# A gated cross-attention and MoE block: residual biases moved into causal steps, norm offsets by one GpSimd product with means that VectorE negates

## The chip, the cores and the metric

The kernel runs on one core of one Trainium2 chip. The metric is the device time of one launch in microseconds (us). TensorE is called PE, VectorE DVE, ScalarE ACT, GpSimd POOL, SyncE SP.

## The reference

For each of 32 sequences of 128 rows and 128 features, in float32:

```python
x = x + tanh(g_x) * attention(layernorm(x), ctx, ctx)        # 16 heads of 8, every row sees every key
x = x + tanh(g_f) * ffn(layernorm(x))
# ffn(y):
q, k = rope(y) @ Wq.T + bq, rope(y) @ Wk.T + bk;  v = y @ Wv.T + bv
x1 = layernorm(y + causal_attention(q, k, v) @ Wo.T + bo) * ln1_w + ln1_b
gates = softmax(x1 @ gate_w.T + gate_b); take the two largest of 8
moe = sum over these two of gate * (x1 @ expert_w.T + expert_b)
return layernorm(x1 + moe) * ln2_w + ln2_b
```

The change touches the two norms inside ffn (the first before ln1_w, the second before ln2_w) and the addition of tanh(g_f) * ln2_b to the residual x.

## The kernel before

**Stages.** Sequences are taken in pairs ("groups", G = 2, GROUPS = 16). A unit is a pair in one of the two attentions: units 0 to 15 are the cross attention of groups 0 to 15, units 16 to 31 the causal attention. A unit has eight tiles (TILES), of four heads of one sequence each. One loop over slots n, written out for every engine, runs both: slot n makes the scores of tile n; step s = n // 8, t = n % 8. Causal step k is step 16 + k. Maxima, exponentials and products with the values follow at fixed lags, and the inputs of a unit are prepared two to four steps ahead. The last slots (DRAIN = 257 and eight more, two tiles in each) empty the pipeline. Then comes the last stage (functions z_...): steps of its own, s = 3 to 21, in which group s gets its output projection and first norm, group s-1 its logits, group s-2 gates and experts, group s-3 its second norm. Each engine runs its own list in a fixed order, written by hand in its body function; semaphores count finished instructions. Groups 0 and 1 and a part of 2 are started earlier, in the functions early(n), between the last slots of the attention.

**POOL in a causal step** (pool_attention, L350 to L383): at t = 0 the four instructions of max_split (L338 to L344) that split the maxima of one sequence into bf16 parts, which PE transposes two slots later (L509), and the same at t = 4; at t = 1 second_row (L284) and the first product of the rotation (L303), which waits for DVE's first_row (L684); at t = 2 two more (L307); at t = 3 the attention bias (L317); at t = 5 and 6 middle_part (L322), which waits for DVE's rests (L697), rotate step 3 (L313) and low_part (L327); at t = 7 the deviation with a power (L277, L280). After these, early(n) is called in each slot.

**Where the residual biases are.** x_all holds the residual x. z_pool's early (L1370) multiplies the rows l2w and l2b by tanh(g_f) at slot DRAIN - 18 = 239 (L1373, two instructions, 128x128) and adds l2b to x_all of one group in each of the slots 240 to 255 (L1377, 128x256 each). The pair of x_all is last read by the causal attention three steps before the unit's own step.

**The two norms.** DVE adds the projection from PSUM to the input (attention_add, L1126), takes statistics (L1133) and moments (L1139: mean and variance). POOL's factor1 (L1334) makes v + eps (L796), its power -1/2 (L798, a tensor_tensor of 128x2 with a tile of -0.5), and then, for groups from 2 on, the offset -mean * rstd in one tensor_scalar for each sequence (L1342, 128x1). ACT's normalise1 (L1035) applies rstd as scale and the offset as bias. For groups 0 and 1 DVE normalises (L1145) from mean and rstd and no offset is made; PE transposes the result (transpose_n, L897), POOL multiplies and adds ln1_w and ln1_b (L1313, L1318). The second norm is alike: experts_add (L1225), statistics and moments (L1233, L1239), factor2 on POOL (L1345, offsets L1353), normalise2 on ACT (L1026), then final on POOL (L1326: times l2w, L1332: plus x_all) and a store by SP. The last two groups are closed by DVE: weigh (L1250) and close (L1259), without offsets.

**The other names.** DVE: maxima L716, shift_logits L1158 and L1161, gated_pairs L1208, gating with L1182 and L1184, gated_sum L1215, experts L1199. ACT: copy_x1 L1018 (transposed x1), gate_experts L1059. PE: logits L909, experts L923, gated_sum L942 and L944, transposes L897, project L886. DVE's and POOL's orders in a step of the last stage are those of the two functions body (L1262, L1356).

## Time and profile before

| | |
|---|---|
| device time, three runs | 441.07, 441.62, 441.66 us; median 441.62 |
| the profiled execution's own time | 441.23 us |
| its span | 439.4 us |
| PE busy | 385.7 us (88%) |
| DVE busy | 369.2 us (84%) |
| POOL busy | 323.3 us (74%) |
| ACT busy | 288.4 us (66%) |
| granted TensorE clock | 0.998 of full speed |

Times inside the profile count from the span's start. A timeline row gives start, duration, engine, line, operation, the tile written and the tiles read with their shapes, and how many instructions are merged in it; in brackets stands the idle time before it and what ended it. The causal attention runs from about 150 to 330 us, the last stage from about 333 us to the end.

### The profile page before, as it was taken

How to read it: one execution, taken by the hardware profiler on the slowest of the kernel's cores; microseconds unless marked ns; L12 is line 12 of the kernel's file. 1: busy time of each engine (PE TensorE's matmuls, PEld its weight loads, DVE VectorE, ACT ScalarE, POOL GpSimd, SP SyncE). 2: the span in 40 equal slices, each digit the busy share in tenths (PEclk: the TensorE clock that was granted, in tenths of full speed). 3: DMA queues.
4: the chain of work that ended last, by engine and by line, in shares of the span. 5: the costliest groups of instructions: out<-in, count | busy, mean ns of one | idle time of the engine just before them, and what ended most of it. 6: DMA issues, size and time to landing. Idle time of an engine off the chain costs nothing.

```text
span 439.4 us, 17671 instructions
## 1 busy us (share of the span) xinstructions
PE 385.7 (88%) x6538; PEld 231.3 (53%) x6538; DVE 369.2 (84%) x1188; ACT 288.4 (66%) x728; POOL 323.3 (74%) x740
## 2 busy tenths in 40 slices
PE   0368888888888899999999999999999999999994
PEld 0134544454444555666666666666655555555541
DVE  6587999999997878888878878877848999999987
ACT  1126777767766766666666666666665788788772
POOL 4456767767778988888888788849823788888884
PEclk9999999999999999999999999999999999999999
DMA  6855686685553333333434343333000000000001
GB/s 163 193 155 160 170 199 169 162 180 145 132 158 101 98 100 105 104 106 104 109 106 125 103 127 100 99 105 96 12 4 2 1 25 13 24 27 12 25 25 48
DMA packets 88037, 42.76 MB, mean 97 GB/s; under 512 B 16000, under 2 KB 87824, under 8 KB 87952
## 3 DMA queue, kind: packets, MB, share of 16 engines
q1 hardware_dynamic: 80864, 39.59, 34.2%
q10 hardware_dynamic: 7088, 2.04, 2.0%
q8 instruction: 53, 0.87, 0.8%
q14 instruction: 32, 0.26, 0.2%
HBM read 5.69 MB, written 2.10 MB: 18 GB/s over the span
## 4 chain that ended last, share of the span: by engine, by line
PE 41%; DVE 6%; ACT 5%; issue 3%; POOL 1%; SPq 1%; DMA 1%; POOLq 0%; ACTq 0%; DVEq 0%
PE s_bank L923 6%; PE u_bank L499 6%; PE st_bank L923 6%; PE s_bank L421 4%; PE s_bank L434 3%; DVE r L697 2%; PE t_bank L413 2%; PE u_bank L944 2%; PE u_bank L942 2%; PE u_bank L909 2%; PE t_bank L407 2%; ACT z_x_t L1018 2%; ACT part L577 1%; PE u_bank L514 1%; PE t_bank L408 1%
## 5 line engine op out<-in xcount | busy, mean ns | idle before, releaser
L716 DVE TENSOR_REDUCE nm<-s_bank 128x4 f32<-128x512 f32 x256 | 171.5, 683 | 36.3 <-PE s_bank L434 34.0
L599 ACT ACTIVATE pt<-st_bank 128x512 f32<-128x512 f32 x250 | 147.5, 602 | 74.0 <-PE st_bank L434 51.6
L434 PE MATMUL s_bank<-qk 64*64 64x128 bf16 (+1 forms) x1584 | 103.5, 220 | 12.1 <-DVE nm L716 5.7
L499 PE MATMUL u_bank<-pt,vaug 128*32 128x128 f32 x2048 | 108.3, 286 | 1.6 <-DVE ao L733 0.2
L434 PE MATMUL st_bank<-qk 64*64 64x128 bf16 (+1 forms) x1540 | 98.2, 218 | 0.0
L434 PEld LDWEIGHTS s_bank<-qk 64*64 64x64 bf16 (+1 forms) x1584 | 73.8, 104 | 36.1 <-issue 18.9
L434 PEld LDWEIGHTS st_bank<-qk 64*64 64x64 bf16 (+1 forms) x1540 | 69.1, 103 | 0.0
L499 PEld LDWEIGHTS u_bank<-pt,vaug 128*32 128x32 f32 x2048 | 41.1, 108 | 27.5 <-issue 5.2
L421 PE MATMUL s_bank<-mqk,idb 64*64 64x256 bf16 x256 | 38.3, 292 | 0.8 <-ACT pt L599 0.4
L327 POOL TENSOR_TENSOR part<-r,part 128x512 bf16<-128x512 f32 x32 | 37.1, 1158 | 1.4
L421 PE MATMUL st_bank<-mkq,idb 64*64 64x256 bf16 x244 | 35.7, 293 | 0.0
L606 ACT ACTIVATE mts<-m_bank 128x128 bf16<-128x128 bf16 x63 | 17.5, 278 | 24.9 <-PE m_bank L509 24.9
L514 PE MATMUL u_bank<-idf,us 128*128 128x128 f32 x128 | 28.0, 300 | 5.2 <-ACT us L615 4.9
L1059 ACT ACTIVATE z_gated<-st_bank,z_gates 128x128 f32<-128x128 f32 x120 | 32.3, 381 | 0.0
L923 PE MATMUL s_bank<-ewt,z_x_t 128*128 128x512 f32 x64 | 31.4, 613 | 0.0
L923 PE MATMUL st_bank<-ewt,z_x_t 128*128 128x512 f32 x64 | 30.2, 594 | 0.0
L338 POOL TENSOR_SCALAR mst<-nm 128x16 bf16<-128x16 f32 x64 | 13.0, 203 | 23.2 <-DVE nm L716 22.9
L322 POOL TENSOR_SCALAR part<-r 128x512 bf16<-128x512 f32 x32 | 19.8, 617 | 13.5 <-DVE r L697 7.3
L421 PEld LDWEIGHTS s_bank<-mqk,idb 64*64 64x64 bf16 x256 | 14.3, 103 | 24.5 <-issue 13.8
L1199 DVE SCALAR_TENSOR_TENSOR z_acc<-s_bank,z_gates,z_acc 128x128 f32<-128x128 f32 x96 | 26.1, 342 | 0.0
L798 POOL TENSOR_TENSOR z_rstd<-z_ve,mhalf 128x2 f32<-128x2 f32 x32 | 23.7, 741 | 2.7
L280 POOL TENSOR_TENSOR rstd<-ve,mhalf 128x2 f32<-128x2 f32 x32 | 22.8, 711 | 2.7
(136 smaller groups left out, 815.4 us busy)
## 6 DMA issues: line engine op xcount, KB each, us to landing
qk<-part SPq DMA_DIRECT2D x221, 128.0 KB, 2.8
x_all<-x SPq DMA_DIRECT2D x16, 128.0 KB, 2.6
qk<-qrow SPq DMA_DIRECT2D x32, 64.0 KB, 2.0
c_all<-ctx_in SPq DMA_DIRECT2D x14, 128.0 KB, 2.8
out<-z_o SPq DMA_DIRECT2D x14, 128.0 KB, 1.8
qk<-mts ACTq DMA_DIRECT2D x34, 32.0 KB, 2.7
qk<-mts SPq DMA_DIRECT2D x30, 32.0 KB, 2.1
ewt<-exp_t SPq DMA_DIRECT2D x1, 512.0 KB
```

Of the source, the lines that this page charges most:

```text
L280: pool.tensor_tensor(rstd[u % 2][:, :], ve[u % 2][:, :], mhalf[:, :], ALU.pow).then_inc(rstd_s, 1)
L327: pool.tensor_tensor(part[u % 2][:, 2:2 * PARTS:PARTS, :], r32[:, :].rearrange("c (o t) -> c o t", o=2), part[u % 2][:, 1:2 * PARTS:PARTS, ...
L421: pe.matmul(to, idb[rows, rows], mask[rows, rows].unsqueeze(1).broadcast_to([64, HEADS, 64]), start=True, stop=False, skip_group_check=True)
L434: ins = pe.matmul(to[outs, :], fixed[:, outs], moving, start=not masked, stop=True, skip_group_check=masked)
L499: ins = pe.matmul(u_bank[b][32 * j:32 * j + 32, r * P:(r + 1) * P], v, pt[m % 4][:, j, :], start=half == 0, stop=half == 1, skip_group_che ...
L514: ins = pe.transpose(u_bank[q % 2][:, W + r * P:W + (r + 1) * P], us[q % 2][:, r * P:(r + 1) * P], idf[:, :])
L599: act.activation(pt[m % 4][:, :, :].rearrange("k j q -> k (j q)"), transposed_bank(m)[:, :], ACT.Exp).then_inc(ex, 1)
L716: dve.tensor_reduce(nm[q % 2][:, first:first + HEADS], s_bank[n % 2][:, :].rearrange("q (j k) -> q j k", j=HEADS), AX_X, ALU.max, negate=T ...
L798: pool.tensor_tensor(r_out, v_eps, mhalf[:, :], ALU.pow).then_inc(semaphore, 1)
L923: ins = pe.matmul(e_bank[b][k][:, :], zx1t[i][:, b * P:(b + 1) * P], ewt[:, k * 512:(k + 1) * 512], start=True, stop=True)
L1059: ins = act.activation(zyg[:, b, e, :], e_bank[b][1][:, e * P:(e + 1) * P], ACT.Copy, scale=zg[i][:, b, HALF + e:HALF + e + 1])
L1199: dve.scalar_tensor_tensor(out=zacc[i][e % 2][:, b, :], in0=e_bank[b][0][:, e * P:(e + 1) * P], scalar=zg[i][:, b, e:e + 1], in1=zacc[i][( ...
```

## The change

The addition of l2b to x_all goes from slots 240 to 255 into earlier ones: groups 0 to 8 at t = 0 of causal steps 4 to 12 (slots 160, 168, ... 224), groups 9 to 13 in slots 232 to 236 (causal step 13), groups 14 and 15 in slots 242 and 246 (step 14). The two products that make l2w and l2b go from slot 239 to slot 152 (causal step 3). DVE gets a new instruction after the moments of each first norm, and of each second norm but the last group's: tensor_scalar of the two means (128x2) by -1 into a new tile. POOL's two tensor_scalars for the offsets become one tensor_tensor of 128x2, negated means times rstd. factor1, factor2 and weigh wait for all instructions on their semaphores, the new one among them. The counts on the semaphores are adapted (H1 and ALL from 5 to 6; the rstd counts from 4 to 3 for each group).

```diff
--- before.py
+++ after.py
@@ -801,7 +801,7 @@
             return [sb(f"{name}{i}", shape) for i in range(2)]
         zo_t = two("z_att_t", [P, W])
         zh = two("z_h", [P, G, P])
-        zst = two("z_stats", [P, G, 6]); zmv = two("z_mv", [P, G, 2]); zve = two("z_ve", [P, G]); zrs = two("z_rstd", [P, G]); znb = two("z_offset", [P, G])
+        zst = two("z_stats", [P, G, 6]); zmv = two("z_mv", [P, G, 2]); zve = two("z_ve", [P, G]); zrs = two("z_rstd", [P, G]); znb = two("z_offset", [P, G]); zmn = two("z_minus_mean", [P, G]); zmn2 = two("z_minus_mean2_", [P, G])
         zn = two("z_n", [P, G, P])
         zw = sb("z_nw", [P, G, P]); zx1 = two("z_x1", [P, G, P])
         zx1t = two("z_x1_t", [P, W])
@@ -822,10 +822,10 @@
         z_gtc = sem("z_gates_t_copied"); z_y = [sem(f"z_experts{k}") for k in range(2)]; z_yg = sem("z_experts_gated"); z_yp = sem("z_gated_pairs_summed"); z_yq = sem("z_gated_summed"); z_yb = sem("z_expert_bias")
         z_acc = sem("z_accumulated"); z_all = sem("z_all_summed_steps"); z_rs2 = sem("z_rstd2_steps"); z_y2s = sem("z_normalised2")
         z_fin = sem("z_final_steps"); z_xb = sem("z_residual_biased"); z_yw = sem("z_weighted"); z_yo = sem("z_closed_by_vector"); z_out = sem("z_stored"); z_tail = [sem(f"z_tail_stored{i}") for i in range(2)]
-        H1 = 1 + 2 * G
+        H1 = 2 + 2 * G
         GATE = 11
         ACC = G * HALF
-        ALL = 1 + 2 * G
+        ALL = 2 + 2 * G
         FIN = 2
         LAST = GROUPS - 1
 
@@ -840,7 +840,10 @@
             return (u_bank[0] if g else t_bank)[:, first:first + G * NE]
 
         def rstd_steps(g):
-            return 2 * g if g <= 2 else 4 * g - 4
+            return 2 * g if g <= 2 else 3 * g - 2
+
+        def all_steps(g):
+            return (g + 1) * ALL - (1 if g == LAST else 0)
 
         def in_z(c, lag):
             return 0 <= c - lag < GROUPS
@@ -1019,7 +1022,7 @@
                                scale=l1wc[:, :]).then_inc(z_x1c, 1)
 
             def normalise2(g, gc):
-                act.wait_ge(z_rs2, (g + 1) * 4)
+                act.wait_ge(z_rs2, (g + 1) * 3)
                 if gc >= 2:
                     act.wait_ge(z_fin, (g - 2) * FIN + 1)
                 for b in range(G):
@@ -1138,6 +1141,12 @@
                 for b in range(G):
                     dve.bn_aggr(zmv[i][:, b, :], zst[i][:, b, :]).then_inc(z_h, 1)
 
+            def attention_minus_mean(g, gc):
+                i = gc % 2
+                dve.wait_ge(z_h, (g + 1) * H1 - 1)
+                dve.tensor_scalar(zmn[i][:, :], zmv[i][:, :, 0], -1.0, 0.0, ALU.mult, ALU.add).then_inc(z_h, 1)
+
+
             def normalise1(g, gc):
                 i = gc % 2
                 dve.wait_ge(z_rs, 2 * (g + 1))
@@ -1149,6 +1158,7 @@
                 attention_add(g, gc)
                 attention_stats(g, gc)
                 attention_moments(g, gc)
+                attention_minus_mean(g, gc)
 
             per_seq = [P, G, NE]
 
@@ -1238,21 +1248,28 @@
                 for b in range(G):
                     dve.bn_aggr(zmv2[g % 2][:, b, :], zst2[g % 2][:, b, :]).then_inc(z_all, 1)
 
+            def experts_minus_mean(g, gc):
+                if g < LAST:
+                    dve.wait_ge(z_all, (g + 1) * ALL - 1)
+                    dve.tensor_scalar(zmn2[g % 2][:, :], zmv2[g % 2][:, :, 0], -1.0, 0.0, ALU.mult, ALU.add).then_inc(z_all, 1)
+
+
             def all_experts(g, gc):
                 experts_add(g, gc)
                 experts_stats(g, gc)
                 experts_moments(g, gc)
+                experts_minus_mean(g, gc)
 
             def weigh(g):
                 i = g % 2
-                dve.wait_ge(z_all, (g + 1) * ALL)
+                dve.wait_ge(z_all, all_steps(g))
                 for b in range(G):
                     dve.scalar_tensor_tensor(out=zyc[i][:, b, :], in0=zsum[i][:, b, :], scalar=zmv2[i][:, b, 0:1],
                                              in1=l2w[:, :], op0=ALU.subtract, op1=ALU.mult).then_inc(z_yw, 1)
 
             def close(g):
                 i = g % 2
-                dve.wait_ge(z_rs2, (LAST - 1) * 4 + (i + 1) * 2)
+                dve.wait_ge(z_rs2, (LAST - 1) * 3 + (i + 1) * 2)
                 dve.wait_ge(z_yw, (i + 1) * G)
                 dve.wait_ge(z_xb, GROUPS)
                 for b in range(G):
@@ -1275,6 +1292,8 @@
                     experts_stats(s - 3, c - 3)
                     attention_moments(s, c)
                     experts_moments(s - 3, c - 3)
+                    attention_minus_mean(s, c)
+                    experts_minus_mean(s - 3, c - 3)
                 elif in_z(c, 3):
                     all_experts(s - 3, c - 3)
                 if in_z(c, 3):
@@ -1307,6 +1326,12 @@
             return early, steps
 
         def z_pool(pool):
+            FIRST_BIAS = (GROUPS + 4) * TILES
+
+            def last_bias(g):
+                pool.tensor_tensor(zpair(x_all, g), zpair(x_all, g), l2b[:, :].unsqueeze(1).broadcast_to([P, G, P]),
+                                   ALU.add).then_inc(z_xb, 1)
+
             def x1(g, gc):
                 i = gc % 2
                 pool.wait_ge(z_n, (g + 1) * G)
@@ -1337,21 +1362,18 @@
                 if gc >= 2:
                     pool.wait_ge(z_n, (g - 1) * G)
                 rstd_of(pool, zmv[i][:, :, 1], zve[i][:, :], zrs[i][:, :], z_rs, rstd_steps(g))
-                for b in range(G if g >= 2 else 0):
+                if g >= 2:
                     pool.wait_ge(z_rs, rstd_steps(g) + 2)
-                    pool.tensor_scalar(znb[i][:, b:b + 1], zmv[i][:, b, 0:1], zrs[i][:, b:b + 1], -1.0,
-                                       ALU.mult, ALU.mult).then_inc(z_rs, 1)
+                    pool.tensor_tensor(znb[i][:, :], zmn[i][:, :], zrs[i][:, :], ALU.mult).then_inc(z_rs, 1)
 
             def factor2(g, gc):
                 i = g % 2
-                pool.wait_ge(z_all, (g + 1) * ALL)
-                k = g * 4 if g < LAST else (LAST - 1) * 4 + 2
+                pool.wait_ge(z_all, all_steps(g))
+                k = g * 3 if g < LAST else (LAST - 1) * 3 + 2
                 rstd_of(pool, zmv2[i][:, :, 1], zve2[i][:, :], zrs2[i][:, :], z_rs2, k)
                 if g < LAST - 1:
                     pool.wait_ge(z_rs2, k + 2)
-                    for b in range(G):
-                        pool.tensor_scalar(znb2[i][:, b:b + 1], zmv2[i][:, b, 0:1], zrs2[i][:, b:b + 1], -1.0,
-                                           ALU.mult, ALU.mult).then_inc(z_rs2, 1)
+                    pool.tensor_tensor(znb2[i][:, :], zmn2[i][:, :], zrs2[i][:, :], ALU.mult).then_inc(z_rs2, 1)
 
             def body(s, c):
                 if in_z(c, 1):
@@ -1368,14 +1390,17 @@
                     factor2(s - 3, c - 3)
 
             def early(n):
-                if n == DRAIN - 18:
+                if n == FIRST_BIAS - TILES:
                     for t in (l2w, l2b):
                         pool.tensor_scalar(t[:, :], t[:, :], tg[:, 1:2], 0.0, ALU.mult, ALU.add).then_inc(c_l2, 1)
                     pool.wait_ge(c_l2, 2)
-                g = n - DRAIN + 17
-                if 0 <= g < GROUPS:
-                    pool.tensor_tensor(zpair(x_all, g), zpair(x_all, g), l2b[:, :].unsqueeze(1).broadcast_to([P, G, P]),
-                                       ALU.add).then_inc(z_xb, 1)
+                g, t = divmod(n - FIRST_BIAS, TILES)
+                if 0 <= g < 9 and t == 0:
+                    last_bias(g)
+                if g == 9 and t < 5:
+                    last_bias(9 + t)
+                if g == 10 and t in (2, 6):
+                    last_bias(14 + t // 4)
                 if n == DRAIN - 4:
                     factor1(0, 0)
                 if n == DRAIN - 2:
```

## Rows read from the trace of the kernel before

**Rows 1.** Busy us: from:to length, PE, PEld, DVE, ACT, POOL, clock, DMA, GB/s

```profile
210.00:230.00 20.00, 19.42 (x486) 12.69 (x485) 16.08 (x40) 13.36 (x30) 16.19 (x36) 1.00 0.39 105
...
360.21:366.82 6.61, 6.40 (x26) 3.59 (x25) 6.19 (x35) 5.37 (x19) 5.67 (x13) 1.00 0.08 22
```

**Rows 2.** Timeline of PE, last stage: start, us, instruction, [idle before <- releaser]

```profile
372.45 0.61 PE L909 MATMUL u_bank<-gwt,z_x_t 128*128 128x8 f32 x4 [0.21 <-ACT z_x_t L1018]
```

**Rows 3.** Chain that ended last, in order of time: start, us, engine, tile, line

```profile
365.85 0.61 PE u_bank L909 x4
...
370.84 0.63 PE u_bank L944 x2
...
371.83 0.57 ACT z_x_t L1018
```

**Rows 4.** Timeline of POOL, causal step 6 (columns as in rows 2)

```profile
220.59 0.22 POOL L344 TENSOR_TENSOR mst<-mr,mst 128x16 bf16<-128x16 f32 x1
220.80 0.80 POOL L284 TENSOR_SCALAR xn_all<-x_all,mv,rstd 128x128 f32<-128x128 f32 x1
...
222.28 0.72 POOL L303 TENSOR_TENSOR rc<-xn_all,cost 128x256 f32<-128x256 f32 x1 [0.69 <-DVE xn_all L684]
...
226.25 0.62 POOL L322 TENSOR_SCALAR part<-r 128x512 bf16<-128x512 f32 x1 [0.55 <-DVE r L697]
```

**Rows 5.** Timeline of PE, between causal and last stage

```profile
316.31 0.44 PE L897 MATMUL t_bank<-idf,z_n 128*128 128x128 f32 x2 [0.95 <-DVE z_n L1145]
```

**Rows 6.** Timeline of DVE, the same stretch

```profile
315.25 1.00 DVE L1145 TENSOR_SCALAR z_n<-z_h,z_mv,z_rstd 128x128 f32<-128x128 f32 x2
...
320.88 0.59 DVE L1145 TENSOR_SCALAR z_n<-z_h,z_mv,z_rstd 128x128 f32<-128x128 f32 x2
```

**Rows 7.** Timeline of POOL, the same stretch

```profile
314.72 1.45 POOL L1377 TENSOR_TENSOR x_all<-x_all,l2b 128x256 f32<-128x256 f32 x2
```

**Rows 8.** Timeline of DVE, causal step 6

```profile
221.86 0.34 DVE L684 TENSOR_SCALAR xn_all<-x_all,mv,rstd 128x128 f32<-128x128 f32 x1
```

**Rows 9.** Timeline of POOL, causal step 13

```profile
294.45 0.20 POOL L338 TENSOR_SCALAR mst<-nm 128x16 bf16<-128x16 f32 x1 [3.31 <-DVE nm L716]
```

**Rows 10.** Timeline of DVE, last stage: its first and a later step

```profile
334.55 0.68 DVE L1208 TENSOR_TENSOR z_gated_pairs<-z_gated 128x512 f32<-128x512 f32 x1
...
367.59 0.17 DVE L1161 TENSOR_REDUCE z_max<-z_logit 128x2 f32<-128x16 f32 x1
...
367.89 0.69 DVE L1208 TENSOR_TENSOR z_gated_pairs<-z_gated 128x512 f32<-128x512 f32 x1
```

**Rows 11.** Timeline of DVE, the end

```profile
428.40 0.77 DVE L1215 TENSOR_TENSOR z_gated_sum<-z_gated_pairs 128x256 f32<-128x256 f32 x1
429.09 0.69 DVE L1182 TENSOR_TENSOR z_top<-z_exps,z_others 128x16 f32<-128x16 f32 x1
...
433.13 0.25 DVE L1239 BATCH_NORM_AGGREGATE z_mv<-z_stats 128x2 f32<-128x6 f32 x2
433.42 0.61 DVE L1250 SCALAR_TENSOR_TENSOR z_yc<-z_x_moe,z_mv,l2w 128x128 f32<-128x128 f32 x2
```

**Rows 12.** Timeline of POOL, last stage: its first and a later step

```profile
334.73 1.06 POOL L798 TENSOR_TENSOR z_rstd<-z_ve,mhalf 128x2 f32<-128x2 f32 x1
...
367.73 0.70 POOL L798 TENSOR_TENSOR z_rstd<-z_ve,mhalf 128x2 f32<-128x2 f32 x1
368.53 0.50 POOL L1342 TENSOR_SCALAR z_offset<-z_mv,z_rstd 128x1 f32<-128x1 f32 x2
```

**Rows 13.** Lines L1182 and L1215 by source: count, duration min/median/max in ns

```profile
L1182 DVE TENSOR_TENSOR z_top<-z_exps,z_others x16: 166/168/692, 325.5 to 429.1; 128x16 f32<-128x16 f32 x16
...
L1215 DVE TENSOR_TENSOR z_gated_sum<-z_gated_pairs x15: 412/415/765, 335.9 to 428.4; 128x256 f32<-128x256 f32 x15
```

**Rows 14.** Timeline of POOL, the end

```profile
428.16 0.73 POOL L1326 TENSOR_TENSOR z_yw<-z_y,l2w 128x256 f32<-128x256 f32 x1
428.97 0.78 POOL L1332 TENSOR_TENSOR z_o<-z_yw,x_all 128x256 f32<-128x256 f32 x1
```

## The prediction

> **What bounds the kernel now.** The page comes first: TensorE is busy for 88% of the span, VectorE for 84%, GpSimd for 74%. Those are averages, so each stage that the change touches is read by itself.
>
> *Last stage.* One step by the view of busy time [rows 1] lasts 6.61 us; PE is busy for 6.40 of them, DVE for 6.19, ACT for 5.37, POOL for 5.67, at full clock. PE's own timeline has one gap in it [rows 2]: 0.21 us ahead of the logits at L909, until ACT has copied z_x_t. The chain that ended last [rows 3] runs from L909 to L909 in 372.45 - 365.85 = 6.60 us through matmuls and that one copy; nothing of POOL, nothing of the norms. The step is PE's 6.40 plus 0.21. The copy starts when PE's own transposes are done, and these stand in PE's order, which is kept.
>
> *Causal stage.* PE bounds it too, 19.42 us busy in 20 [rows 1]. POOL has two waits in a step [rows 4], 0.69 us before L303 (for DVE's first row, L684) and 0.55 us before L322 (for the rests, L697): 1.24 us to spare in 10.03 us (a step is the distance of equal rows).
>
> *Passage.* At 316.31 PE stands for 0.95 us [rows 5], waiting for DVE's z_n (L1145). DVE was working all along: it reached L1145 at 315.25 and took 1.00 us for the two [rows 6]; the same two at 320.88 took 0.59. The difference, 0.41 us, falls while POOL runs two residual biases (314.72, 1.45 us) [rows 7].
>
> **The change, part by part.**
>
> *Biases moved, causal steps 4 to 12.* Nine TENSOR_TENSORs of 0.72 us (1.45 / 2, rows 7) go behind the first maxima split of a step. Before, L344 starts at 220.59 and L284 directly behind it; now L284 starts about 0.7 later, at 221.5, and ends at 222.3. DVE's L684 [rows 8] was done at 222.20 and L303 waited for it until 222.28. So the 0.69 gap swallows the bias, if L684 isn't held. L684 starts at 221.86, when L284 is now at work; z_n beside the biases shows that a tensor_scalar of DVE can be held. Held to L284's end, it finishes 0.35 us later, about 222.55; L303 starts 0.35 late, and the 0.55 gap before L322 takes that. Of 1.24 us, 0.72 + 0.35 = 1.07 are used. PE doesn't notice. Cost taken: 0; bounds 0 and, if the cover were gone, the whole excess in each of nine steps (second rival). The Trainium skill ("SBUF — State Buffer", Who interferes with whom) states that VectorE in a 2-port mode, or with two SBUF inputs against a reading GpSimd instruction, and GpSimd exclude each other for the whole instruction. By it the hold here is certain rather than possible, and the sum is the same 0, since the figure above already holds L684 to the end of L284.
>
> *Causal step 13.* Five biases, 3.6 us. Four lie in the 3.31 us for which POOL waits before the split at 294.45 [rows 9], 2.9 us. The fifth lies between a split and L322, where rows 4 have 0.55 us: at most 0.17 late, once. The stacks' issues on SP follow two more instructions of POOL; I take 0, bound +0.17. *Step 14:* two biases and the l2w, l2b pair (moved to slot 152, where it stands in a causal step as a bias does, two instructions with half the elements each) leave a stretch in which POOL ran without a pause and PE too. Nothing on SP's queue is moved past; the moved work issues no DMA. 0.
>
> *What leaves the passage.* The sixteen biases, the last of them up to 316.2 [rows 7], are gone from here. POOL is idle beside z_n(0), so the pair takes 0.59 instead of 1.00: -0.41. PE waits for exactly this (0.95 us), and what follows on PE and on POOL (L1313, then the last maxima split) follows z_n.
>
> *VectorE's negated means.* Nothing shows a 128x2 tensor_scalar on DVE. Nearest rows: L1161, which writes 128x2, takes 0.17 [rows 10]. With the 0.04 us by which a waiting DVE instruction follows the one before (L1239 ends at 433.38, L1250 starts at 433.42) [rows 11] that is 0.21. Lower bound 0, if it slips into a wait; upper bound twice that, 0.42. I take 0.21, as the shape is the same. Where it counts:
> - Step 0 in the passage: it stands between the moments of group 0 and the maxima and z_n behind them on DVE, which run without idle up to 315.25 [rows 6]: +0.21. POOL's rstd comes 0.21 later too, still ahead of z_n. So PE gets z_n(0) at -0.41 + 0.21 = **-0.20**.
> - Steady steps: two of them, the first hidden behind the second moments' pipeline, so about 0.25 us in all, in front of L1158 and L1161. L1161 ended at 367.76 and L1208 started at 367.89, when ACT's z_gated was there. DVE is busy for 6.19 of 6.61 us: 0.42 to spare. The maxima of the logits come 0.2 later, so do ACT's exponentials, and DVE's chain gives at most 0.05, before z_h (L1126), which waits for PE anyway. 0 per step.
> - The end: weighing of group 14 (L1250) waits one more instruction, on the path that ends: **+0.21**.
>
> *GpSimd's product.* Two tensor_scalars of 128x1, 0.50 us together [rows 12], become one tensor_tensor of 128x2. Nearest row: L344's tensor_tensor of 128x16, 0.22 [rows 4]; from above, L798 at the same shape with a power, 0.70 (bounds 0.2 and 0.7). I take 0.22: -0.28 per norm. But the rstd now waits for the negated mean, +0.2, so that the first offsets come about when they did (369.03), and the second some 0.3 earlier. Behind them stand ACT's normalisations, z_n which PE transposes only behind L944 (370.84 [rows 3]). In steady steps nothing of it reaches PE: 0.
>
> There is a trap in it. The power at L798 starts at 367.73 and L1208 (two SBUF inputs) at 367.89, and neither is stretched; at 334.73 L1208 had begun first (334.55 [rows 10]), and the same power took 1.06 [rows 12]. With L796 0.2 later the power comes behind L1208: +0.36 on POOL. By the skill's rule above one of the two would have to wait for the other in every step; rows 10 and 12 show both at their usual length when the power is first, so here the measurement decides. POOL has 0.9 us to spare in a step, so 0 either way.
>
> *The end.* L1215 and L1182 took 0.77 and 0.69 us at 428.40 and 429.09 [rows 11], against medians of 0.415 and 0.168 [rows 13]. They end where POOL's L1326 (428.16 + 0.73) and L1332 (428.97 + 0.78) end or get going [rows 14]: DVE is held by GpSimd's last products. These follow the offsets of group 13; these come 0.28 earlier with one product (0.2 of it certain), and L1182 is released that much earlier: **-0.22**.
>
> **Sum:** -0.20 (passage) - 0.22 + 0.21 (end) = -0.2 us. The profiled execution took 441.23 us (span 439.4 and 1.8 around it), 0.39 below the median of the runs, 441.62. On its own scale that is 441.0; on the median's 441.4.
>
> **Rivals.**
> - *The holds at the end go altogether* (L1215 and L1182 at their medians: -0.36 - 0.52 = -0.88 instead of -0.22), and ACT's copy of group 15 comes 0.12 earlier: -0.20 - 0.88 - 0.12 + 0.21 = -1.0, 440.6. For it: POOL is earlier. Against it: L1326 and L1332 back to back last 1.5 us, and an advance of 0.3 doesn't carry them past DVE.
> - *The hold in the causal steps outgrows its cover*: place, L684 behind the bias; price, whatever the bias and the hold take beyond 1.24 us, as the parts, the rstd and the next maxima split then come late and PE waits at L509. It decides from 0.17 us more hold than I charge. At 0.2 us of excess, nine steps give +1.8: 443.2, slower. For it: z_n(0) was held though the first bias had ended. Against: behind L284 POOL waits for L684 itself, so nobody can hold it further.
> - *The relief doesn't come* (L1145 takes 1.00 for another reason): +0.21 instead of -0.20, and with +0.21 - 0.22 at the end 441.8: no difference that shows.
> - *DVE becomes the bound of the last stage*: from 0.42 us for the two new instructions on. At 0.3 each, 0.18 over in 13 steps: +2.3, 443.9. Against: nothing that small takes 0.3 on DVE.
>
> **How the numbers follow.** Forecast 0.58, holds gone 0.14, cover outgrown 0.07, no relief 0.16, DVE bound 0.05. A measurement of this kernel tells 0.2% (0.88 us) from nothing. Faster by more: most of the second case, 0.12. Slower by more: the third and the fifth, 0.12. Within: 0.76. The range goes from the second case, 440.6, to "no relief" with twice the price of the negated means (+0.21 at both places) and 0.17 in step 13, 442.3; the two slow cases, 0.12, stay outside.
>
> **What would show it.** Right: L1145 at 0.59 in its first pair, PE's wait at L897 0.75 instead of 0.95; equal distances of L909 in the last stage; L303's wait near 0 and L322's at 0.2 with steps of 10.03; L1182 released some 0.2 earlier; new DVE rows of some 0.17. Wrong: a causal step longer than 10.03, idle time of PE at L509 behind L344, or a last-stage step other than 6.60.

## The result, and the profile after

The changed kernel takes 442.53 us (median of 9 runs, 442.03 to 442.77), the one before 441.13 on the same chip (9 runs, 440.81 to 441.66); the ratio is 1.0025 with a 95% interval of 1.0016 to 1.0034. So it is slower, by 0.16 to 0.34%, and 442.53 lies 0.23 us above the range. The profiled execution took 442.59 us with a span of 440.8 (before 441.23 and 439.4). Ratios here and below are given with their 95% interval; they are estimates over all runs and differ a little from the quotient of two medians, which is 1.0032 here.

The change shifts the line numbers. What was L897, L909, L923 and L1018 is L900, L912, L926 and L1021 in the changed kernel; DVE's L1182, L1199, L1208, L1215 and L1225 are L1192, L1209, L1218, L1225 and L1235; POOL's L1342 and L1353 are L1367 and L1376, its L1326 and L1332 are L1351 and L1357. L1332 is now the residual bias, and L1225 the sum of gated pairs.

**Causal stage.** POOL's timeline of step 6 in the changed kernel; compare [rows 4].

```profile
220.12 0.22 POOL L344 TENSOR_TENSOR mst<-mr,mst 128x16 bf16<-128x16 f32 x1
220.29 0.72 POOL L1332 TENSOR_TENSOR x_all<-x_all,l2b 128x256 f32<-128x256 f32 x1
221.01 0.85 POOL L284 TENSOR_SCALAR xn_all<-x_all,mv,rstd 128x128 f32<-128x128 f32 x1
222.00 0.72 POOL L303 TENSOR_TENSOR rc<-xn_all,cost 128x256 f32<-128x256 f32 x1
...
225.77 0.62 POOL L322 TENSOR_SCALAR part<-r 128x512 bf16<-128x512 f32 x1 [0.35 <-DVE r L697]
```

The bias (L1332) stands where L284 stood, L303's wait of 0.69 is gone and 0.35 is left before L322. DVE's first row (L684) is not held, as the same step of DVE's timeline shows: it starts while L284 is at work and takes 0.34 us, as before. L284 took 0.85 instead of 0.80. The step is 10.03 us long as before.

```profile
221.38 0.34 DVE L684 TENSOR_SCALAR xn_all<-x_all,mv,rstd 128x128 f32<-128x128 f32 x1
```

**Passage.** PE's and DVE's timelines there; compare [rows 5, 6].

```profile
315.82 0.44 PE L900 MATMUL t_bank<-idf,z_n 128*128 128x128 f32 x2 [0.59 <-DVE z_n L1154]
```

```profile
313.41 0.17 DVE L1147 TENSOR_SCALAR z_minus_mean<-z_mv 128x2 f32<-128x2 f32 x1
315.17 0.59 DVE L1154 TENSOR_SCALAR z_n<-z_h,z_mv,z_rstd 128x128 f32<-128x128 f32 x2
```

Both terms are there: z_n is down from 1.00 to 0.59, and a negated mean of 0.17 stands in front of it. From the matmuls of project(0) to the transposes of z_n(0) PE needs 5.47 us instead of 5.67.

**Last stage.** The distance of one step's logits from the next was 6.60 us in the steady steps (the first took 6.50, the last 6.47). In the changed kernel 6.76 and 6.60 take turns. Rows of one long step, from all engines, around the norms and the logits that end it (compare [rows 2, 10, 12]):

```profile
367.23 0.15 DVE L1147 TENSOR_SCALAR z_minus_mean<-z_mv 128x2 f32<-128x2 f32 x1
...
367.47 0.19 POOL L796 TENSOR_SCALAR z_ve<-z_mv 128x2 f32<-128x2 f32 x1 [0.92 <-DVE z_minus_mean L1147]
...
367.71 0.69 DVE L1218 TENSOR_TENSOR z_gated_pairs<-z_gated 128x512 f32<-128x512 f32 x1
...
367.75 1.22 POOL L798 TENSOR_TENSOR z_rstd<-z_ve,mhalf 128x2 f32<-128x2 f32 x1
...
369.04 0.48 POOL L1367 TENSOR_TENSOR z_offset<-z_minus_mean,z_rstd 128x2 f32<-128x2 f32 x1
369.05 0.41 DVE L1225 TENSOR_TENSOR z_gated_sum<-z_gated_pairs 128x256 f32<-128x256 f32 x1
...
369.90 0.69 POOL L798 TENSOR_TENSOR z_rstd<-z_ve,mhalf 128x2 f32<-128x2 f32 x1
...
370.67 0.20 POOL L1376 TENSOR_TENSOR z_offset<-z_minus_mean,z_rstd 128x2 f32<-128x2 f32 x1
...
370.89 0.88 ACT L1029 ACTIVATE z_y<-z_x_moe,z_offset,z_rstd 128x128 f32<-128x128 f32 x2 [0.20 <-POOL z_offset L1376]
...
371.68 0.25 ACT L1052 ACTIVATE z_gates_t<-u_bank 16x128 f32<-16x128 f32 x1
371.84 0.54 ACT L1021 ACTIVATE z_x_t<-t_bank,l1bc,l1wc 128x256 f32<-128x256 f32 x1
...
372.43 0.39 PE L912 MATMUL u_bank<-gwt,z_x_t 128*128 128x8 f32 x2 [0.37 <-ACT z_x_t L1021]
```

Read it from top to bottom. v+eps (L796) waits for the negated mean, so the power starts 0.04 us behind DVE's L1218, and takes 1.22 us instead of 0.70. The product then starts as DVE's L1225 does, and takes 0.48. The second norm follows in POOL's order. Its product ends at 370.87, which is 5.20 us behind the logits (at 365.67) instead of 4.90. ACT's z_y was waiting for it. Behind z_y stand, in ACT's order, the copies of the gates and of x1, and PE waits for the copy of x1: 0.37 us instead of 0.21. The chain of waits, which before held no instruction of any norm [rows 3], now goes through z_y:

```profile
371.30 0.15 ACT z_y L1029
...
371.70 0.23 ACT z_gates_t L1052
371.93 0.46 ACT z_x_t L1021
```

In the next step things fall out differently. The negated mean comes 6.60 us behind the one before (373.83), but DVE's L1218 6.69 us, so the first norm's power gets in 0.05 us ahead of it and takes 0.70; its product takes 0.20. The second norm's power starts 0.01 us ahead of DVE's L1225 and takes 0.98, yet its offsets end 4.50 us behind the logits (at 372.43), early enough. Rows of POOL, then of DVE:

```profile
374.35 0.70 POOL L798 TENSOR_TENSOR z_rstd<-z_ve,mhalf 128x2 f32<-128x2 f32 x1
375.12 0.20 POOL L1367 TENSOR_TENSOR z_offset<-z_minus_mean,z_rstd 128x2 f32<-128x2 f32 x1
...
375.68 0.98 POOL L798 TENSOR_TENSOR z_rstd<-z_ve,mhalf 128x2 f32<-128x2 f32 x1
```

```profile
373.83 0.15 DVE L1147 TENSOR_SCALAR z_minus_mean<-z_mv 128x2 f32<-128x2 f32 x1
...
374.40 0.69 DVE L1218 TENSOR_TENSOR z_gated_pairs<-z_gated 128x512 f32<-128x512 f32 x1
...
375.69 0.41 DVE L1225 TENSOR_TENSOR z_gated_sum<-z_gated_pairs 128x256 f32<-128x256 f32 x1
```

So long steps of 6.76 and short ones of 6.60 take turns; twelve steps last 80.18 us instead of 79.23: **+0.95**. The view by source line gives the powers of both norms over the whole stage, in the kernel before and then in the changed one (count: shortest/median/longest in ns):

```profile
L798 POOL TENSOR_TENSOR z_rstd<-z_ve,mhalf x28: 699/734/1057, 334.7 to 426.9; 128x2 f32<-128x2 f32 x28
```

```profile
L798 POOL TENSOR_TENSOR z_rstd<-z_ve,mhalf x28: 688/838/1218, 334.4 to 427.7; 128x2 f32<-128x2 f32 x28
```

**The end.** PE's and DVE's timelines; compare [rows 11].

```profile
425.89 0.69 PE L912 MATMUL u_bank<-gwt,z_x_t 128*128 128x8 f32 x4 [1.04 <-ACT z_x_t L1021]
426.44 3.57 PE L926 MATMUL s_bank<-ewt,z_x_t 128*128 128x512 f32 x4
```

```profile
429.16 0.46 DVE L1225 TENSOR_TENSOR z_gated_sum<-z_gated_pairs 128x256 f32<-128x256 f32 x1
429.54 0.69 DVE L1192 TENSOR_TENSOR z_top<-z_exps,z_others 128x16 f32<-128x16 f32 x1
430.26 0.17 DVE L1194 TENSOR_TENSOR z_gates<-z_top,z_rsum 128x16 f32<-128x16 f32 x1
...
430.88 0.61 DVE L1209 SCALAR_TENSOR_TENSOR z_acc<-s_bank,z_gates,z_x 128x128 f32<-128x128 f32 x2 [0.44 <-DVE z_gates L1194]
...
434.29 0.17 DVE L1254 TENSOR_SCALAR z_minus_mean<-z_mv 128x2 f32<-128x2 f32 x1
```

Four things: the last logits come 6.76 us behind those of the step before (in the kernel before 6.47), +0.29; DVE's sum of gated pairs (L1225, before L1215) took 0.46 instead of 0.77, -0.31; the negated mean of group 14, +0.21; and 0.44 us for which DVE stands idle before L1209, of which 0.09 were there before, +0.35. In this execution the granted clock also fell, to 0.50, the lower of its two levels (1.2 of 2.4 GHz), for some 3 us behind PE's wait of 1.04, and L926 took 3.57 us instead of 1.96. Busy time by windows of 1 us, the columns those of [rows 1]:

```profile
425.00:426.00 1.00, 0.11 (x1) 0.11 (x1) 0.96 (x4) 1.00 (x5) 0.92 (x3) 1.00 0.00 0
...
427.00:428.00 1.00, 1.00 (x2) 0.34 (x1) 0.69 (x4) 1.00 (x6) 0.80 (x3) 0.50 0.00 0
```

### The profile page after: what moved, and what is told of

It is laid out like the page before. It is cut to its first block, busy times and chain, and to the rows that moved or that the text cites. A ratio compares the mean times of both kernels' runs of the same rounds, so it can differ in the third digit from the quotient of the medians.

```text
span 440.8 us, 17675 instructions
## 1 busy us (share of the span) xinstructions
PE 386.7 (88%) x6538; PEld 232.0 (53%) x6538; DVE 372.4 (84%) x1219; ACT 286.9 (65%) x728; POOL 321.9 (73%) x712
## 4 chain that ended last, share of the span: by engine, by line
PE 45%; ACT 5%; DVE 4%; issue 3%; POOL 1%; POOLq 0%; ACTq 0%; DVEq 0%
PE u_bank L499 7%; PE s_bank L926 7%; PE st_bank L926 6%; PE s_bank L421 4%; PE s_bank L434 4%; DVE r L697 2%; PE u_bank L947 2%; PE u_bank L945 2%; PE t_bank L413 2%; PE u_bank L912 2%; PE t_bank L407 2%; ACT z_x_t L1021 2%; PE u_bank L514 1%; ACT part L577 1%; PE t_bank L408 1%
## 5 line engine op out<-in xcount | busy, mean ns | idle before, releaser
L926 PE MATMUL s_bank<-ewt,z_x_t 128*128 128x512 f32 x64 | 33.0, 641 | 0.0
L926 PE MATMUL st_bank<-ewt,z_x_t 128*128 128x512 f32 x64 | 30.2, 594 | 0.0
L798 POOL TENSOR_TENSOR z_rstd<-z_ve,mhalf 128x2 f32<-128x2 f32 x32 | 28.0, 875 | 2.7
L322 POOL TENSOR_SCALAR part<-r 128x512 bf16<-128x512 f32 x32 | 19.8, 618 | 10.8 <-DVE r L692 6.3
L796 POOL TENSOR_SCALAR z_ve<-z_mv 128x2 f32<-128x2 f32 x32 | 6.4, 201 | 29.0 <-DVE z_minus_mean L1147 23.9
L1209 DVE SCALAR_TENSOR_TENSOR z_acc<-s_bank,z_gates,z_acc 128x128 f32<-128x128 f32 x96 | 26.1, 342 | 0.0
```

What stands on the lines that cost most here:

```text
L322: pool.tensor_scalar(part[u % 2][:, 1:2 * PARTS:PARTS, :], r32[:, :].rearrange("c (o t) -> c o t", o=2), 1.0, 0.0, ALU.mult, ALU.add).then ...
L798: pool.tensor_tensor(r_out, v_eps, mhalf[:, :], ALU.pow).then_inc(semaphore, 1)
L926: ins = pe.matmul(e_bank[b][k][:, :], zx1t[i][:, b * P:(b + 1) * P], ewt[:, k * 512:(k + 1) * 512], start=True, stop=True)
L1209: dve.scalar_tensor_tensor(out=zacc[i][e % 2][:, b, :], in0=e_bank[b][0][:, e * P:(e + 1) * P], scalar=zg[i][:, b, e:e + 1], in1=zacc[i][( ...
```

## The experiments

The queue theory: v+eps waits for the negated mean, so POOL's norms come later, and ACT's queue, its instructions in their fixed order, passes that on to PE. The rivals: DVE's two extra instructions delay its own chain; the moved biases cost; and, once the trace showed it, the clock at the end. "Before" is the kernel before, run beside each experiment again. A letter in a quoted expectation is defined in that text. The step of the last stage is the distance of one step's logits from the next.

**1. The biases alone**, all of the change in `early` and nothing else:

```diff
-                if n == DRAIN - 18:
+                if n == FIRST_BIAS - TILES:
...
+                g, t = divmod(n - FIRST_BIAS, TILES)
+                if 0 <= g < 9 and t == 0:
+                    last_bias(g)
...
```

> The kernel before with only the biases (and the l2w, l2b pair) moved; no negated means. Theory A (the loss lies in the last stage: POOL's powers start 0.2 us later, get behind DVE's gated_pairs, and the late second offsets delay ACT's copy_x1): the last-stage steps stay 6.60 us, z_n's pair takes 0.59, and the passage is shorter; against before -0.2 to -0.4 us. Theory B (the biases in the causal steps cost something that later waits show): slower than before by some of the +1.3 us that the change cost.

Measured: 440.78 us, 0.9992 [0.9983, 1.0001]. z_n takes 0.59, from project(0) to the transposes 5.25 us (-0.42), and every steady step of the last stage is 6.60. The time alone does not tell this kernel from the one before; its trace has the saving that was forecast, and no cost.

**2. The norms alone**, the biases where they stood:

```diff
-                if n == FIRST_BIAS - TILES:
+                if n == DRAIN - 18:
...
+                g = n - DRAIN + 17
+                if 0 <= g < GROUPS:
```

> The changed norms with the biases left at slots 240 to 255. Theory A: the full loss and no gain of the passage: every second step of the last stage 6.76 instead of 6.60 us, +1.3 to +1.7 us against before. Theory B: within 0.3 us of before.

Measured: 443.05 us, 1.0036 [1.0023, 1.005]. z_n takes 1.00 again, the steps are 6.77 and 6.60 in turn, twelve of them 80.22 us. The loss is the norms'.

**3. The powers don't wait.** All of the change, but v+eps and power of both norms wait for the moments only, and the product alone waits for the negated mean:

```diff
             def factor1(g, gc):
-                pool.wait_ge(z_h, (g + 1) * H1)
+                pool.wait_ge(z_h, (g + 1) * H1 - 1)
...
                     pool.wait_ge(z_rs, rstd_steps(g) + 2)
+                    pool.wait_ge(z_h, (g + 1) * H1)
...
             def factor2(g, gc):
-                pool.wait_ge(z_all, all_steps(g))
+                pool.wait_ge(z_all, (g + 1) * ALL - 1)
...
                     pool.wait_ge(z_rs2, k + 2)
+                    pool.wait_ge(z_all, all_steps(g))
```

> The changed kernel, but v + eps and the power wait for the moments alone, and only the product waits for the negated means. DVE's instructions are all there. Theory A: the power starts ahead of gated_pairs again and takes 0.70 in every step, all steps 6.60, so about 1.2 us faster than the changed kernel, 0.1 to 0.3 faster than before. Theory C (DVE's own two instructions make the steps longer, by way of the logits' maxima): the steps of 6.76 stay, and the time is the changed kernel's.

Measured: 441.12 us, 0.9992 [0.9983, 1.0001], all steady steps 6.60. The two extra instructions of DVE are still there, so they cost the steps nothing. POOL's and ACT's rows of the step at 365.90 in this kernel:

```profile
367.50 0.19 POOL L796 TENSOR_SCALAR z_ve<-z_mv 128x2 f32<-128x2 f32 x1 [1.04 <-DVE z_mv L1142]
367.77 0.70 POOL L798 TENSOR_TENSOR z_rstd<-z_ve,mhalf 128x2 f32<-128x2 f32 x1
...
370.58 0.87 ACT L1029 ACTIVATE z_y<-z_x_moe,z_offset,z_rstd 128x128 f32<-128x128 f32 x2
...
371.66 0.27 ACT L1052 ACTIVATE z_gates_t<-u_bank 16x128 f32<-16x128 f32 x1 [0.21 <-PE u_bank L935]
371.88 0.56 ACT L1021 ACTIVATE z_x_t<-t_bank,l1bc,l1wc 128x256 f32<-128x256 f32 x1
```

Here z_y is early and ACT waits 0.21 us for PE ahead of the gates, so the norm has that much to spare. In the kernel before, the three followed each other without a wait: nothing to spare.

```profile
370.79 0.88 ACT L1026 ACTIVATE z_y<-z_x_moe,z_offset,z_rstd 128x128 f32<-128x128 f32 x2
371.61 0.27 ACT L1049 ACTIVATE z_gates_t<-u_bank 16x128 f32<-16x128 f32 x1
371.83 0.56 ACT L1018 ACTIVATE z_x_t<-t_bank,l1bc,l1wc 128x256 f32<-128x256 f32 x1
```

POOL's only wait of more than 0.1 us in that step lay ahead of the two norms:

```profile
367.45 0.19 POOL L796 TENSOR_SCALAR z_ve<-z_mv 128x2 f32<-128x2 f32 x1 [0.33 <-DVE z_mv L1139]
```

**4. POOL later, in the kernel before.** A spare 128 x 2 tensor_scalar ahead of the first norm's v+eps, and no other part of the change:

```diff
+                if g >= 3:
+                    pool.wait_ge(z_dum, g - 3)
+                    pool.tensor_scalar(zdum[:, :], zmv[i][:, :, 1], 1.0, EPS, ALU.mult, ALU.add).then_inc(z_dum, 1)
```

> The kernel before with one spare tensor_scalar of 128x2 (0.19 us) on POOL ahead of v + eps of the first norm, groups 3 to 15; nothing on DVE. Theory A: the power falls behind gated_pairs and is stretched by 0.3 to 0.5 us, and with the two tensor_scalars for each norm still there the second offsets come 0.5 us late: each last-stage step 0.3 to 0.55 longer, +3.6 to +6.6 us. Theory C: POOL has 0.9 us to spare in a step, so the time is that of before (within 0.3 us).

Measured: 451.43 us, 1.0248 [1.0226, 1.027], +10.1 us and more than either theory expected. Most steps take 7.30 to 7.38 us. One near the start takes 6.61, and two take 8.29 and 8.07, where the granted clock fell to 0.50 for some 3 us. POOL's rows:

```profile
369.42 0.19 POOL L1341 TENSOR_SCALAR z_spare<-z_mv 128x2 f32<-128x2 f32 x1
...
369.98 1.18 POOL L798 TENSOR_TENSOR z_rstd<-z_ve,mhalf 128x2 f32<-128x2 f32 x1
371.26 0.74 POOL L1345 TENSOR_SCALAR z_offset<-z_mv,z_rstd 128x1 f32<-128x1 f32 x2
```

One instruction of 0.19 us costs 0.7 us a step: the power falls behind DVE here too (+0.48), and the pair of offsets is held as well (0.74 instead of 0.50). Of the added 0.28 + 0.48 + 0.24 = 1.0 us, 0.7 reach PE.

**5. Only the first norm's powers don't wait**, the part of experiment 3's edit in factor1:

> The changed kernel, with only the first norm's v + eps and power waiting for the moments alone; the second norm waits as in the change. Theory A says that the one wait that decides is the first norm's, since POOL comes to the second norm long after its negated means: all steps 6.60, the time of the run in which both were freed (441.1, 0.9992 of before). Rival: each norm's wait costs its share, steps of 6.68 in every second place, about 441.8.

Measured: 440.97 us, 0.9996 [0.9986, 1.0006], steady steps 6.60, powers at 0.70 and 0.69. The wait of the second norm costs nothing, since POOL gets to it only when its mean has long been there.

**6. Second offsets later, in the kernel before.** A spare 128 x 2 tensor_scalar between the two norms; nothing of the first is touched, DVE has nothing more to do, and no power is stretched (longest 1.055 us, as before):

```diff
+                    if s >= 4:
+                        pool.wait_ge(z_dum, s - 4)
+                        pool.tensor_scalar(zdum[:, :], mhalf[:, :], 1.0, EPS, ALU.mult, ALU.add).then_inc(z_dum, 1)
```

> The kernel before with one spare 128 x 2 instruction on POOL between the first norm's and the second norm's work of each last-stage step; nothing of the first norm is later. Theory A (ACT's queue has no slack: the second offsets release normalise2, behind it stand the copy of the gates and then the copy of x1, on which PE's logits wait): the second offsets come about 0.28 us later (spare 0.19 and its issue), and the whole of it or most of it reaches PE: logits 6.75 to 6.9 apart instead of 6.60, over 13 steps 2 to 3.7 us, so 443.1 to 444.8 us. Rival B (ACT is busy for 5.4 of 6.6 us and has slack; only the first norm's lateness or DVE's extra 0.4 us matter): logits stay 6.60 apart, 441.1 +- 0.4.

Measured: 442.9 us, 1.0035 [1.0023, 1.0047], steps of 6.71 or 6.72 from the third on: twelve last 80.55 us, +1.32. Its PE row

```profile
372.88 0.61 PE L909 MATMUL u_bank<-gwt,z_x_t 128*128 128x8 f32 x4 [0.32 <-ACT z_x_t L1018]
```

shows 0.32 against 0.21 [rows 2]. The offsets end 5.14 us behind the logits instead of 4.90, and of these 0.24 us half arrives, 0.12. The direction of the queue theory is shown, the size that I gave it was too large: against the logits z_y starts 0.24 us later than before, the gates' copy 0.20 and the copy of x1 0.14, so each link of ACT's queue takes up some of it.

**7. No unused negated means.** Experiment 3, and the means that nobody multiplies (groups 0 and 1 of the first norm, 14 of the second) aren't negated; the negations count on semaphores of their own:

```diff
-        H1 = 2 + 2 * G
+        H1 = 1 + 2 * G
...
+                if g >= 2:
...
-                if g < LAST:
+                if g < LAST - 1:
```

> Powers wait for the moments alone, and DVE leaves out the negated means that nobody reads (groups 0 and 1 of the first norm, group 14 of the second). My prediction priced these at 0.21 each on the path, in the passage (group 0) and at the end (group 14). If so: 0.3 to 0.4 us faster than the run with both powers freed, 440.7, 0.998 of before; z_h to z_n(0) 2.80 us instead of 3.01. Rival: they stand beside other waits, no difference from that run.

Measured: **440.15 us**, 0.9977 [0.9968, 0.9985]: faster than both kernels. By its trace against that of before: -0.41 in the passage, steps unchanged at 6.60, -0.09 at the last of them, -0.28 from the last logits to the end (10.86 us to DVE's last row instead of 11.14), together -0.78. Against experiment 5, measured beside it, the time is 0.82 us shorter, more than the 0.42 that I charged for the two unused means: DVE's idle 0.35 us is gone too (at the end experiment 5 needs 11.41 us).

**8. PE filled, and 9. the change once more.** The changed kernel with three spare matmuls in the gap ahead of its last logits, and the changed kernel itself beside it:

```diff
+                if s - 1 == LAST:
+                    pe.wait_ge(z_h, LAST * H1 + 1)
+                    for b in (0, 1, 0):
+                        pe.matmul(m_bank[:, b * P:(b + 1) * P], zo_t[1][:, b * P:(b + 1) * P], wo[:, :], start=True, stop=True)
```

> The changed kernel with three more matmuls of 128x128 on PE, their output not used, in the gap of 1.04 us ahead of the last logits. In the profiles of the change PE's granted clock is 0.5 for some 3 us from about there, and the four matmuls of s_bank take 3.4 us instead of 1.8. Theory D: the fall follows PE's idle time there and costs 0.6 to 0.8 us at the end; with the gap filled the clock stays at 1.00 and the time is 0.5 to 0.8 us below the change's (441.8). Rival: the fall comes and goes by itself, no difference.

> The changed kernel once more, beside the other runs of this call, and a second profile of it. Theory A: alternate steps of 6.60 and 6.76, 1.0 to 1.5 us above before. Theory D: the granted clock falls near the last logits in this profile too.

Measured: 442.32 us, 1.0025 [1.0016, 1.0034], and 442.45, 1.0027 [1.0018, 1.0037]. In the filled kernel the clock is 1.00 up to 432. So it is in the second profile of the change, although PE was idle for as long (1.03 us):

```profile
424.00:428.00 4.00, 2.96 (x14) 1.76 (x13) 3.86 (x16) 3.53 (x13) 3.65 (x7) 1.00 0.02 4
428.00:432.00 4.00, 4.00 (x13) 1.73 (x11) 3.25 (x17) 2.62 (x11) 3.54 (x7) 1.00 0.20 62
```

From the last logits to DVE's last row it needs 11.39 us there and 11.94 where the clock fell: the fall costs 0.55 us in an execution that has it. But this one without it took 442.50 us, like the median of 442.45, so the loss is there without the clock; and the filling bought nothing that can be told. The second profile, being free of the fall, is the one used for the account below.

**10. Experiment 7 with the biases where they stood before** (the diff of experiment 2), so the norms' share alone:

> The version of the change without waits of the powers and without the unused negated means, but with the residual biases where they stood before: tells how much of that version's gain each part brings. If the biases carry it (my reading of the passage: z_n 1.00 against 0.59 us, 0.42 us for both): time between that version's 440.15 and the kernel before, near 440.6, and z_n takes 1.00 again with 5.67 us from project to transposes. If the norms carry it: 440.2, as that version. If the norms' part is worth nothing: 441.1.

Measured: 440.83 us, 0.9986 [0.9978, 0.9995]; z_n takes 1.00, and the passage is 22.32 us long from project(0) to the first logits (before 22.30, experiment 7 21.88). By the traces somewhat over half of experiment 7's gain is the biases', the rest the norms', and that comes at the end. The intervals of the two times overlap, so the times alone don't give the split.

**11. Experiment 7 with the unused mean of group 14 back:**

```diff
-                if g < LAST - 1:
+                if g < LAST:
```

> The version without waits and without unused negated means, with the one unused negated mean of group 14 put back (at the end, where DVE sets the pace). Theory A (0.17 us and its issue on the path, nothing else): 0.21 us longer from the last logits to the end (10.86 becomes 11.07), time 440.35. Rival (the 0.35 us for which DVE stood idle ahead of its first accumulation, in every version with all the negated means counted in the semaphores of the norms, comes with this instruction): 11.42 us, time 440.7.

Measured: 440.72 us, 0.9984 [0.9975, 0.9993]; 10.95 us at the end instead of 10.86. The time is the one that the rival expected, but against the kernel before the ratio can't be told from experiment 7's, and the trace speaks against the rival: the idle 0.35 us of DVE does not come back, so it isn't this instruction's. It is in the traces of the change (both) and of experiments 2, 3, 5 and 8, and in none of the kernel before, 1, 4, 6, 7, 10 and 11. Those that have it count the negations on the semaphores of the moments and also negate the unused means of groups 0 and 1; no run separates the two. Why it is there stays open.

## Why the prediction was wrong

From the traces of the kernel before and of the change in experiment 9, in us to DVE's last row: passage, from project(0) to the first logits, 22.11 - 22.30 = -0.19; thirteen steps 86.68 - 85.73 = +0.95; last logits 6.77 - 6.47 = +0.30; end 11.39 - 11.14 = +0.25. Sum +1.3; the spans differ by 440.7 - 439.4 = +1.3. The start of project(0) isn't in this sum: over the thirteen traces it lies between 310.35 and 311.64 us, wherever the biases stand.

The miss is larger than the 0.23 us above the range. The forecast started from 441.62, the median of three runs; over nine the kernel before took 441.13. Forecast was -0.2 us, measured +1.4. The top of the range is also 0.1 low by its own terms: 441.8 + 0.42 + 0.17 is 442.4, not 442.3, which 442.53 lies above as well.

- *Biases in causal steps 4 to 14, 0:* right. The wait before L303 took the bias, as worked out. L684 was not held at all (0.34), so less of the cover was used than I charged. (Held to L284's end at 222.32 and then at its full 0.34, L684 would have ended at 222.66, not 222.55; 1.18 of the 1.24 us would still have covered it.) The prediction took the hold as certain by the Trainium skill ("SBUF — State Buffer", Who interferes with whom). That section says it of VectorE in a 2-port mode or with two SBUF inputs, and frees an instruction with one SBUF input outside these modes. L684 has one SBUF tensor as input; no run here shows its mode. It starts inside L284 and is not longer, so the trace does not agree if it was in a 2-port mode.
- *Passage, -0.20:* right in both terms. From project(0) to the first logits experiment 1, the biases alone, has 21.90 us, -0.40; experiment 2, the norms alone, 22.54, +0.24. The "no relief" rival is out.
- *Negated mean at 0.17 and its issue, 0.21:* right, 0.15 and 0.17 in the steady steps. But "nothing that small takes 0.3 on DVE" was wrong for the one at 426.63, beside POOL's L1357: 0.68. It cost nothing there, since DVE still waited 0.27 us for ACT before L1218. "0 per step" for its time on DVE: right, shown by experiment 3.
- *GpSimd's product, 0.22:* 0.20 where nothing is beside it. But the sentence that has the first offsets "about when they did" and the second "some 0.3 earlier" counted neither the stretched power nor a stretched product, though a stretch of 0.36 was foreseen a few lines on; it was 0.52. In the trace the product of the long step ends at 369.52, 3.85 us behind the logits instead of 3.18, and the second one 0.30 later instead of 0.3 earlier.
- **The step that failed:** "In steady steps nothing of it reaches PE: 0", and "POOL has 0.9 us to spare in a step, so 0 either way". Its root stands at the start: "The copy starts when PE's own transposes are done". That chain was read as if it named the only condition. The copy of x1 stands in ACT's queue behind z_y and the gates' copy, z_y waits for POOL's second offsets, and in the kernel before all three were back to back (370.79, 371.61, 371.83): the copy was bound by both, and the chain names one. Of POOL's 0.9 us of idle time the only wait in one piece, 0.33 us, lies ahead of the norms, and the rest are gaps of 0.1 us or less between instructions; a late start of the norm isn't taken up by it. The price is 0.16 us in every second step, +0.95, and with the same cause +0.30 at the last logits (PE idle 1.03 instead of 0.75). Experiments 3 and 5, which free the power from the wait, bring every steady step back to 6.60 and the last one to 6.38 and 6.39.
- *End, -0.22 and +0.21:* the hold shrank, by 0.31, at the sum of gated pairs (L1215, now L1225) rather than at L1182; the negated mean cost 0.21; and DVE's idle 0.35 us came on top, which no row of before shows. This part of the loss, a quarter of the +1.3, has no cause shown.
- None of the rivals was this one. "DVE becomes the bound" had the right instructions and the wrong engine: it is POOL that waits for them, and ACT that hands the delay on. That the change is slower at all was given 0.12, by ways that the runs don't show.

## What to carry to other kernels

Before an edit that makes an engine later, follow its output not to the bound engine but to every queue on the way: an instruction that the bound engine waits for may stand, in order, behind one that waits for yours, and a chain of waits shows only one of two tied conditions. Add a wait at the last instruction that needs it, not at the head of the group: here, moving it from v+eps to the product turned +0.25% into no difference that can be told (0.9992 and 0.9996), and leaving out the results that nobody reads as well made it 0.23% faster. Look at which of two engines' instructions starts first where one can stretch the other: POOL's power stood 0.16 us ahead of DVE's L1208, and a shift of 0.20 us made the first offsets 0.67 us late, three times itself.

## What the runs showed of the hardware

In the last stage a power of 128 x 2 on GpSimd took 0.70 us when it started 0.04 us or more ahead of VectorE's L1208/L1218 (two SBUF inputs, 0.69 us) and 1.05 to 1.22 when it started 0.03 to 0.2 us behind; VectorE's instruction took 0.68 to 0.70 either way. Beside VectorE's shorter L1225 (0.41 us) the second norm's power took 0.98 although its record starts 0.01 us earlier. The single product of 128 x 2 took 0.20, and 0.48 when it started together with L1225.

The Trainium skill ("SBUF — State Buffer", Who interferes with whom) says that of two such instructions the one issued second waits for the other whole instruction. The trace agrees in the main when GpSimd is second (the power of 1.22 us ends 0.57 us behind VectorE's L1218), and not when it is first.

VectorE's 128 x 2 negation took 0.15 to 0.17, and 0.68 once in each profile of the change, at 426.63 in the first, beside GpSimd's L1357, although it reads 2 elements per partition.

The granted clock fell near the end in one of two profiles of the same kernel, with PE idle for 1.04 and 1.03 us ahead of the last logits. In experiment 4, PE was idle for 0.91 to 0.98 us ahead of ten of the logits, and the clock fell behind two of them. So idle time of that length doesn't decide it alone. The two steps with a fall took 0.8 to 1.0 us longer than their neighbours.
